# AdaLN block on one core: weight scaling moved behind the transposition, its split shared out over VectorE, ScalarE and GpSimd

## What is computed

```
mod = silu(c) @ wmod                     # six rows of 512 per batch: sa, ca, ga, sb, cb, gb
gb  = (2 * (gb >= 0) - 1) * max(|gb|, 0.25)
x   = x + ga * attention(h)              # only rows 0 to 15 of a batch depend on the heads;
                                         # all others get ga * bo
h   = layernorm(x) * (1 + cb) + sb
xd, wd = quantise(h), quantise(weight)   # to a grid of 6-bit floats, in blocks of 32, and back
x   = x + gb * (xd @ wd.T + bias)
```

## Time and profile before

| | |
|---|---|
| median of 3 executions | 370.23 us (369.77 to 370.35) |
| the profiled execution's own time | 371.03 us |
| its span in the profile | 369.1 us |
| busy: TensorE matmul, VectorE, ScalarE, GpSimd | 90%, 79%, 60%, 59% of the span |
| mean granted TensorE clock | 0.976 of full speed |

### The profile page before, as it was taken

How to read it: one execution, slowest core, us unless ns; L and a number is a source line. 1 busy time by engine, 2 the same in 40 slices (tenths; PEclk the granted TensorE clock), 3 DMA queues, 4 the chain that set the end, 5 groups by cost and what they waited for, 6 DMA issues and landing times.

```text
span 369.1 us, 6369 instructions
## 1 busy us (share of the span) xinstructions
PE 330.8 (90%) x2334; PEld 251.7 (68%) x2334; DVE 290.8 (79%) x508; ACT 223.0 (60%) x505; POOL 216.9 (59%) x131
## 2 busy tenths in 40 slices
PE   3987999549999799989999999989999989995894
PEld 1232556438988686777888678768877877684783
DVE  4799949998448996879798689896976989699732
ACT  3367654765756867786778588948593875121210
POOL 2068392462886679559967796898684767402000
PEclk9999899997999999999999999999998999998999
DMA  7989999975197727965697669768681982020122
GB/s 219 404 333 360 295 231 223 322 269 100 69 201 175 186 114 134 265 101 197 150 275 194 174 135 262 179 168 170 230 198 37 222 174 115 3 99 17 67 103 85
DMA packets 22933, 66.93 MB, mean 181 GB/s; under 512 B 2371, under 2 KB 2500, under 8 KB 18934
## 3 DMA queue, kind: packets, MB, share of 16 engines
q1 hardware_dynamic: 15360, 51.83, 41.8%
q0 software_dynamic: 7392, 14.68, 24.2%
q10 hardware_dynamic: 150, 0.02, 0.0%
HBM read 49.39 MB, written 17.14 MB: 180 GB/s over the span
## 4 chain that ended last, share of the span: by engine, by line
PE 43%; DVE 36%; ACT 10%; issue 8%; DMA 1%; DVEq 0%; SPq 0%; ACTq 0%
PE ps L679 7%; PE ps L680 7%; PE ps L684 7%; DVE XL L1107 5%; PE ps L660 4%; DVE Q L1148 4%; DVE WL L1114 3%; DVE amax L1129 3%; ACT U L447 3%; PE ps L763 3%; DVE X L1162 3%; PE ps L623 3%; DVE DD L1155 3%; ACT XH L430 2%; ACT unused L460 2%
## 5 line engine op out<-in xcount | busy, mean ns | idle before, releaser
L370 POOL TENSOR_TENSOR U<-U,c_bc 128x1024 f32<-128x1024 f32 x31 | 75.6, 2439 | 48.3 <-ACT U L447 48.2
L679 PE MATMUL ps<-WH,XH 128*128 128x512 f32 x256 | 103.4, 404 | 0.3 <-ACT XH L430 0.3
L680 PE MATMUL ps<-WL,XH 128*128 128x512 f32 x256 | 103.0, 402 | 0.0
L430 ACT ACTIVATE XH<-ps 128x512 fp32r<-128x512 f32 x64 | 37.8, 591 | 84.8 <-PE ps L660 84.6
L1107 DVE TENSOR_TENSOR XL<-ps,XH 128x512 fp32r<-128x512 f32 x64 | 43.9, 686 | 52.8 <-ACT XH L430 52.7
L377 POOL TENSOR_TENSOR U<-U,sb_bc 128x1024 f32<-128x1024 f32 x31 | 74.1, 2389 | 4.5 <-POOL U L370 0.2
L684 PE MATMUL ps<-WH,XL 128*128 128x512 f32 x256 | 68.8, 390 | 0.0
L447 ACT ACTIVATE U<-X,nmr,rstd 128x512 f32<-128x512 f32 x64 | 48.2, 807 | 24.7 <-DVE nmr L1122 21.5
L680 PEld LDWEIGHTS ps<-WL,XH 128*128 128x128 f32 x256 | 49.9, 195 | 11.5
L679 PEld LDWEIGHTS ps<-WH,XH 128*128 128x128 f32 x256 | 50.1, 196 | 9.5 <-ACT XH L430 0.6
L684 PEld LDWEIGHTS ps<-WH,XL 128*128 128x128 f32 x256 | 48.4, 189 | 10.5
(11 more groups left out here) (219 smaller groups left out, 447.9 us busy)
## 6 DMA issues: line engine op xcount, KB each, us to landing
X<-in_x SPq DMA_DIRECT2D x16, 1024.0 KB, 8.5
out<-X SPq DMA_DIRECT2D x15, 1024.0 KB, 5.7
X<-mod_scratch POOLq DMA_DIRECT2D x14, 1024.0 KB, 12.8
X<-in_wmod SPq DMA_DIRECT2D x2, 1024.0 KB, 14.1
sb_bc<-mod_scratch SPq DMA_DIRECT2D x7, 256.0 KB, 12.1
c_bc<-mod_scratch SPq DMA_DIRECT2D x7, 256.0 KB, 10.5
X<-in_wmod SPq DMA_DIRECT2D x2, 512.0 KB, 4.7
Wd<-in_w SPq DMA_DIRECT2D x1, 1024.0 KB, 10.0
```

The lines of the kernel that those rows point to most:

```text
L370: nc.gpsimd.tensor_tensor(a, a, spread(c_bc[:, b % 2, :]), ALU.mult).then_inc(u_done, 2 if g == 0 else 1)
L679: M(bank, XH[:, n % 2, r], WH[:, b % 2, k, :], start=False, stop=False)
L680: M(bank, XH[:, n % 2, r], WL[:, b % 2, k, :], start=False, stop=False)
```

## The change

For batches 2 to 7 the order is turned round. The plain quantised weights are turned once, in slots 7 to 10 (`PLAIN`), and ScalarE keeps them in Wb (`keep_plain`). For each batch TensorE then spreads the row gb[b] over all 128 partitions of W_BANK with a single matmul, at the end of slot 12 for batch 2 and of slot 8b-7 for the others (`SPREAD`). In the two slots after it VectorE multiplies two quarters each by that bank, into Wd (`scale_turned`), and ScalarE makes the two high parts, each as soon as its quarter is scaled. GpSimd forms the four low parts after `modulate` of group 2b+1 (`low_weights`), where before it scaled weights after that group's `from_grid`. Batch 8 takes its parts from Wb in slots 57 to 60 without a turn. Batches 0 and 1 stay as they were. A small DMA brings the rows of gb back into SBUF; VectorE splits them into GG in slot 9.

```
+PLAIN = {7 + k: k for k in range(NC)}
+SPREAD = {12 if b == 2 else 8 * b - 7: b for b in range(2, B)}
 # SyncE
+                if t == 1:
+                    sp.wait_ge(columns_out, 16)
+                    sp.dma_start(gb_rows, mod_dram[GB]).then_inc(bo_in, 16)
 # GpSimd
+            nc.gpsimd.memset(GG[:].bitcast(F32), 0.0).then_inc(cleared, 1)
+            def low_weights(b):
+                pool.wait_ge(wt_low, NC * b)
+                pool.wait_ge(y_done, 8 * (b - 1))
+                for k in range(NC):
+                    pool.wait_ge(wt_high, NC * b + k + 1)
+                    nc.gpsimd.tensor_tensor(WL[:, b % 2, k, :], Wd[:, k, :], WH[:, b % 2, k, :].bitcast(F32),
+                                            ALU.subtract).then_inc(wt_low, 1)
                 modulate(g)
+                if g % 2 == 1 and g >= 5:
+                    low_weights(g // 2)
                 if g - 1 > FILLING:
                     from_grid(g - 1)
-                if g % 2 == 1 and 3 <= g < GROUPS - 1:
-                    scale_weights((g + 1) // 2, Wscaled)
 # ScalarE, weight_high(b, k, bank)
-                if k == 0 and b >= 2:
-                    act.wait_ge(y_done, 8 * (b - 1))
+                if b >= 2:
+                    if k == 0:
+                        act.wait_ge(y_done, 8 * (b - 1))
+                    if b < B:
+                        act.wait_ge(wscaled, NC * b + k + 1)
+                    else:
+                        act.wait_ge(plain_cp, NC)
+                    A.activation(WH[:, b % 2, k, :], turned(b, k), ACT.Identity).then_inc(wt_high, 1)
+                    return
+            def keep_plain(k):
+                act.wait_ge(wt_mm, NC * 2 + k + 1)
+                act.wait_ge(q_mm, 1)
+                A.copy(Wb[:, k, :], ps[:, W_BANK, :]).then_inc(plain_cp, 1)
 # ScalarE, in slot q after high_part(q + 1)
-                if q - 1 in FOLDS:
+                if q - 1 in FOLDS and FOLDS[q - 1][0] in (1, B):
                     weight_high(*FOLDS[q - 1], W_BANK)
+                if q - 1 in PLAIN:
+                    keep_plain(PLAIN[q - 1])
+                for n in (1, 2):
+                    if q - n in SPREAD:
+                        for k in range(2 * n - 2, 2 * n):
+                            weight_high(SPREAD[q - n], k, W_BANK)
 # TensorE, at the end of slot q
+                if q in PLAIN:
+                    weight_turn(2, PLAIN[q], W_BANK)
+                if q in SPREAD:
+                    b = SPREAD[q]
+                    pe.wait_ge(g_rows, 6)
+                    if b == 2:
+                        pe.wait_ge(plain_cp, NC)
+                    else:
+                        pe.wait_ge(wscaled, NC * b)
+                    M(ps[:, W_BANK, :], pick[:, b:b + 1].to_broadcast([P, P]), GG[:], start=True, stop=True
+                      ).then_inc(gb_mm, 1)
 # VectorE, in slot q after low_part(q + 1)
+            def scale_turned(b, k0):
+                dve.wait_ge(gb_mm, b - 1)
+                dve.wait_ge(plain_cp, NC)
+                dve.wait_ge(wt_low, NC * b)
+                for k in range(k0, k0 + 2):
+                    TT(turned(b, k), ps[:, W_BANK, :], Wb[:, k, :], ALU.mult).then_inc(wscaled, 1)
+                for n in (1, 2):
+                    if q - n in SPREAD:
+                        scale_turned(SPREAD[q - n], 2 * n - 2)
+                if q == 9:
+                    gate_rows_split()
```

More of the change, by code:

```diff
@@ L70, in build @@
         TA = sb("TA", [P, NC, COLUMNS, B])
+        GG = sb("GG", [P, D], F32R)
         s32 = sb("s32", [P, 2, NB * HALF])
@@ L126, in build @@
         column_rows = msp[0:COLUMNS * B, 2, :]
+        gb_rows = msp[0:B, 1, :]
         sb_rows, c_rows_all = msp[0:B, 3, :], msp[0:B, 0, :]
@@ L149, in build, with turned @@
         sign, size = by_column(gate_sign[:]), by_column(own[:, 352:384])
+        def turned(b, k):
+            return Wb[:, k, :] if b == B else Wd[:, k, :]
         def mods(i):
@@ L180, in build @@
                 "rows_turned", "columns_cp", "columns_out", "sb_out", "c_out", "g_rows", "u_first",
-                "h_first", "c_heads", "xd1_done", "s32_done"))
-        bd_done, hs_sa = sem("bd_done"), sem("hs_sa")
+                "h_first", "xd1_done", "s32_done"))
+        bd_done, hs_sa, plain_cp, gb_mm = (sem(n) for n in ("bd_done", "hs_sa", "plain_cp", "gb_mm"))
         (exp_c, silu_done, mod_mm, wd_done, wscaled, wt_mm,
@@ L616, in weight_turn @@
             def weight_turn(b, k, bank):
-                if b < B:
+                if b < 2:
                     pe.wait_ge(wscaled, NC * (b + 1))
-                if b > 0:
-                    pe.wait_ge(wt_low, NC * b + k)
-                src = Wfirst if b == 0 else Wsecond if b == 1 else Wscaled if b < B else Wplain
+                if b == 1:
+                    pe.wait_ge(wt_low, NC + k)
+                if b == 2:
+                    if k == 0:
+                        pe.wait_ge(wt_low, NC * 2)
+                    else:
+                        pe.wait_ge(plain_cp, k)
+                src = (Wfirst, Wsecond, Wplain)[b]
                 for c in range(NC):
@@ L628, in _ @@
             rows_of(0, GATE_ROWS)
-            pe.wait_ge(cleared, 3)
+            pe.wait_ge(cleared, 4)
             pe.wait_ge(rows_ok, 2)
@@ L813, in _ @@
             pe.wait_ge(columns_cp, 1)
-            pe.wait_ge(g_rows, 3)
+            pe.wait_ge(g_rows, 4)
             for k in range(NC):
@@ L827, in _ @@
                     pe.wait_ge(hs_sa, 1)
-                if q in FOLDS:
+                if q in FOLDS and FOLDS[q][0] == 1:
                     weight_turn(*FOLDS[q], W_BANK)
+                if q in PLAIN:
[3 more added lines that the diff above has]
+                    pe.wait_ge(g_rows, 6)
+                    if b == 2:
+                        pe.wait_ge(plain_cp, NC)
+                    else:
+                        pe.wait_ge(wscaled, NC * b)
+                    M(ps[:, W_BANK, :], pick[:, b:b + 1].to_broadcast([P, P]), GG[:], start=True, stop=True
+                      ).then_inc(gb_mm, 1)
         @block.vector
@@ L1113, in weight_low, with gate_rows_split @@
                 dve.wait_ge(wt_high, NC * b + k + 1)
-                TT(WL[:, b % 2, k, :], ps[:, bank, :], WH[:, b % 2, k, :].bitcast(F32),
+                TT(WL[:, b % 2, k, :], turned(b, k) if b >= 2 else ps[:, bank, :], WH[:, b % 2, k, :].bitcast(F32),
                    ALU.subtract).then_inc(wt_low, 1)
+            def gate_rows_split():
+                dve.wait_ge(bo_in, 32)
+                W_.tensor_copy(GG[0:B, :], gb_rows).then_inc(g_rows, 1)
+                dve.wait_ge(g_rows, 5)
+                TT(GG[32:32 + B, :], gb_rows, GG[0:B, :].bitcast(F32), ALU.subtract).then_inc(g_rows, 1)
+            def scale_turned(b, k0):
[4 more added lines that the diff above has]
+                    TT(turned(b, k), ps[:, W_BANK, :], Wb[:, k, :], ALU.mult).then_inc(wscaled, 1)
             def scales(g):
```

21 lines of the change are left out of this document (8 added, 13 removed).

## The result

The changed kernel takes 378.98 us (median of 4, 378.81 to 380.57) against 370.14 us (median of 4) before: a ratio of 1.0207, 95% interval 1.0157 to 1.0257. It is slower by 8.8 us. The profiled execution took 379.03 us, its span is 377.2 us, 8.1 more than before. Medians are over all executions of a kernel, ratios leave out those over 1.5% above its fastest, which touches scale_first (4 of 10) and late_plus (1 of 4).

What follows compares the result with a forecast made beforehand. TensorE was taken to set the pace over long stretches. Batch 3 +4.1, batch 7 +2.8, batches 2, 4, 5, 6 +0.2 and batch 8 -2.4 made +4.7 us: 374.9 us on the median, range 363 to 380.

Steps and rivals of the forecast that it cites:

- ScalarE's wait: Slots with scalings: the two high parts, queued behind XH, wait for VectorE's XL and scalings, in sum 2.5 us a slot.
- What TensorE is spared: 24 turns fewer (-10.3 us), six spreading matmuls more (1.5): net -8.8 us; with the waits for WL, -20.4 at best.
- VectorE net 0: On VectorE 24 scalings replace 24 low parts at the same price, so net 0.
- Batch 3: Slots 18 and 19: late high parts delay XH of tile 20 and modulate(7); tile 24 comes 4.1 us late.
- the link that sets tile 24: GpSimd's four low parts behind modulate(7), 1.2 us each, end at 181.7; tile 24's bias matmul waits 3.8 us.
- TensorE's own path: Batch 3 if GpSimd is early: 3.9 us at tile 20 less spared turns and waits, a floor of 1.1 us late.
- rival C: Stalls at tiles 20, 24, 52 and 53 could each bring a fall of TensorE's clock: 379 us; chance 0.08.
- Batch 7: Slots 50 and 51: late high parts delay XH of tile 52 and att; tile 53's bias matmul is 2.8 us late.
- Batches 2, 4, 5, 6: Relief of 8.6 us on TensorE against 8.8 us of ScalarE delay: net +0.2 us, range -8.6 to +11.
- I spread them evenly: The 6.6 us of TensorE's waits split evenly over six batches, giving 4.4 us to batches 2, 4, 5 and 6.
- Batch 8: Slots 57 to 60, VectorE's stretch: without turns TensorE needs only the add there, -2.4 us (bounds 0 and -6.7).
- A: TensorE stays the bound and ScalarE's waits lie in its slack: 361.4 us, at best 349.8; chance 0.30.

Runs made afterwards that it cites:

- scale_first: Changed kernel with VectorE's two scalings of a slot ahead of XL of the next tile instead of behind it: 370.84 us, ratio 0.9951.
- late_plus: late_high with TensorE's matmul for dn one slot later, and att's turn and copy one slot later too (53 and 54): 367.88 us, ratio 0.9876.
- late_high: Changed kernel with ScalarE's two high parts of a scaled pair made one slot later: 368.34 us, ratio 0.9913.
- fill: Changed kernel with TensorE kept busy by repeated bias matmuls (tiles 20, 37, 52) and unused matmuls before its waits for dn and att: 380.06 us, ratio 1.0214.
- short_low: Changed kernel with GpSimd's low parts over 128 of 512 columns, the rest of WL left unformed: 377.81 us, ratio 1.0157.
- low_on_vector: Changed kernel with the low parts of batches 2 to 7 on VectorE again instead of GpSimd: 392.99 us, ratio 1.0577.

## Why the prediction came out as it did

It said slower, 374.9 us (363 to 380), and it is 378.98: the sign and the main mechanism, ScalarE's wait, are right, the sum is too small, +8.8 instead of +4.7 us (on the profiled executions +8.0).

- **What TensorE is spared (-8.8 us, with waits -20.4 at best).** The sizes hold. Slots with a turn before and nothing else go from 3.85 to 3.87 us down to 3.41 or 3.42 (11, 14, 21, 27, 29), the predicted 0.43; slots with a spread are 0.19 to 0.27 longer (17, 25, 33, 41, 49), predicted 0.24. Turns wait 18.1 - 5.1 = 13.0 us less for WL, predicted 11.6. Of -20.4, all slots but the five keep -8.3, though: in some slots a turn less is worth nothing (slot 28 lost its turn and takes 5.64 us where it took 5.42, slot 13 takes 5.78 where it took 5.44).
- **VectorE net 0.** 680 ns a scaling, as taken; right.
- **ScalarE's wait (2.5 us a slot, some 25 us in all).** 25.4 us in 12 waits. late_high takes the wait away and with it 10.6 us between the medians. Shown.
- **Batch 3 (+4.1 us).** Measured over slots 17 to 23: +5.6, the term most mis-sized. The place is right, XH of tile 20 came 5.2 us later (163.77, forecast 162.45): VectorE's XL before it was 1.4 us later than before (155.78 against 154.42), which I had left where it was. But the loss came over GpSimd only in a small part. Tile 21's bias matmul was 5.57 us late (171.45), tile 24's 5.48 (183.42): all of it is in slot 20. The low parts, which I had as the link that sets tile 24, only take up what three turns less give back: one took 1.29 us, priced at 1.2; TensorE waits 1.0 us for them at tile 24, and slot 23 takes 4.68 us in place of 3.42. What I had as "TensorE's own path", the floor of 1.1 us, was the one that decided. Its price was too low for two reasons. The stall at tile 20 is 4.5 us where I had 3.5; as 1.2 us of idle time that slot 20 had before are gone in it, TensorE idles 4.46 instead of 1.19 us there, 3.3 more. And TensorE is busy for 7.55 us in slot 20 at a clock of 0.72, where the same work takes 4.84 at 1.00 in late_high: the fall of the clock, my rival C, came on top with 2.7 us (2.3 against the 5.25 us before, which still held a turn).
- **Batch 7 (+2.8 us).** Slots 49 to 54 lost 3.3. Slot 49 began 6.7 us later than before; counted from there XH of tile 52 moved by 4.2 us (forecast 4.9), the end of att by 4.5 (forecast 5.2), and tile 53's bias matmul by 2.8 (forecast 3.4). Slot 53 then took 1.0 us more at its lower clock, although its turn was gone. Right.
- **Batches 2, 4, 5, 6 (+0.2 us).** Measured +1.0, as slots 7 to 16: -0.2, 24 to 31: -0.7, 32 to 39: +4.6, 40 to 48: -2.6. That the sum looks near is luck. The step behind it, "I spread them evenly" and one average delay a batch, is the one that failed. Batch 5's +4.6 is a thing I had not named: the second pass's dn stands in slot 37, a VectorE instruction with two SBUF inputs that now meets a GpSimd instruction at its start, 2.73 us instead of 1.09; then a stall of 2.8 us and a clock of 0.57 in slot 38. And batch 6's gain holds 2.0 us of slot 46, which happened to run at full clock now. That dn meets GpSimd at its start is lasting: in all ten traces of the new order in which it reads two SBUF tiles it takes 2.55 to 2.80 us.
- **Batch 8 (-2.4 us).** Slots 55 to the end gave -2.0. Slot 57, 7.80 to 5.60 us, gives 2.2 of it, and slot 59, at 4.37 instead of 3.86, takes 0.5 back. Right.
- **The rivals.** A (TensorE stays the bound, 361.4) asked for XH of tile 20 to move by under 0.5 us; it moved by 5.2. With late_high, which takes the waits away, the kernel does get faster, but stops at 368.3 us; 361.4 was not reached by any order tried. C (falls of the clock, 379) is the time that came, yet it was not an alternative to the forecast but came on top of it, and I gave it 0.08. While TensorE has work, its clock falls to half speed in seven places after and in four before.

By terms the sum was 3.3 us short on the profiled executions (+8.0 against +4.7): batch 3 by 1.5, batches 2, 4, 5 and 6 by 0.8, batch 7 by 0.5, batch 8 by 0.4. The rest is the start: slot 0 begins 0.8 us later and slots 0 to 6 take 0.6 less, which I had at 0 and which differs as much between traces of the new order (slot 5 takes 8.70 to 10.17 us in them). Open are why the clock falls in slots 15 and 16 or 46 in some executions and not in others, with TensorE busy, and what brings the slow stretch in slots 40 and 41 when that of slot 38 is gone.

## What to carry over

When work is handed from one engine to another in the same slot, take the result up one slot later: here a wait in the middle of a queue, 25.4 us in sum, cost 10.6 us of time though the engine was only 60% busy, because XH and the exponential stood behind it. A forecast by averages hides exactly this; list, batch by batch, what long piece of the schedule each moved piece meets. And allow for a slow stretch behind every longer stall that you forecast on a full TensorE, as a term with a chance: behind waits of 2.8 us or more in slot 37 it came nine times of nine and cost 1.1 to 2.8 us, behind waits of 2.1 to 2.2 us at the end of slot 52 three times of five.

## What the runs showed of the hardware

- A VectorE instruction with two SBUF inputs and a GpSimd instruction that reads SBUF nearly exclude each other: 2.73 and 2.83 us in the two timelines instead of 0.69. Away from GpSimd two SBUF inputs cost nothing extra: 13 of 24 took 0.68 us, as with one. An instruction's price depends on where its operands lie and on what another engine does at the time.
- GpSimd's low part took 1286 ns over 512 columns and 460 ns over 128: by these two sizes an estimated 2.15 ns a column and some 185 ns fixed.
- The clock fell for fill, short_low and low_on_vector in slots 15 and 16, and in four of 13 traces in slot 46, while TensorE was busy almost all through (14.64 of 15.00 us in fill's window). TensorE: Matmul & The Clock Gate of the Trainium skill (Part 1) ties the lower clock to an idle TensorE. Slot 38, behind a long wait in nine traces, agrees with that; these stretches are not explained by it.
